# Graph-layer stack, one core: scores for four heads in one phase, a slope column in the weights, and sums of two key tiles for the products with ones

## The reference

```python
# layer 0: one GAT head, width 128, slope 0.2;  layer 3: four GAT heads of width 256 and an output GAT, slope 0.01
Wh = x @ W;  f, g = Wh @ a[0], Wh @ a[1]          # one number for each node
e = leaky_relu(f[:, None] + g[None, :]);  e = where(adj > 0, e, -1e9)
out = softmax(e) @ Wh
# layer 1: ordinary attention, 8 heads of width 32
scores = (q @ k.T) / sqrt(32);  scores = where(adj == 0, -inf, scores)
out = softmax(scores) @ v;  out = out @ Wo.T + bo
# layer 2: degree * (x @ Wi.T + b) + adj @ (x @ Wj.T)
# layer 3 goes on with elu, a two-layer FFN, a residual sum and a layernorm with gamma and beta
x = layernorm(x + layer(x))                        # four times
```

## Time and profile before

| what | before |
|---|---|
| median of 3 runs | 3322.02 us (3321.67 to 3324.13) |
| profiled execution, its own time | 3321.83 us |
| its span, first to last instruction | 3320.0 us |
| mean granted TensorE clock | 0.947 |
| PE busy | 2850.9 us, 86% |
| DVE busy | 2056.8 us, 62% |
| ACT busy | 1230.9 us, 37% |
| POOL busy | 811.2 us, 24% |

### The profile page before, as it was taken

The page is one execution under the profiler, slowest core; times in us unless marked ns, Lnnn a source line. Parts: engine busy times, 40 slices in busy tenths (PEclk is TensorE's granted clock), DMA queues, the critical chain, the costliest instruction groups (busy, mean ns, idle before and its releaser), DMA issues. The chain is left out here.

```text
span 3320.0 us, 47744 instructions
## 1 busy us (share of the span) xinstructions
PE 2850.9 (86%) x17559; PEld 2092.7 (63%) x17668; DVE 2056.8 (62%) x5644; ACT 1230.9 (37%) x2273; POOL 811.2 (24%) x640
## 2 busy tenths in 40 slices
PE   0779989898898989899898998989898898989876
PEld 0456666667666676676657666665766666676664
DVE  3447574766747576574857658485665848567453
ACT  0224334352433434343343434334243433424332
POOL 0112131412213132221313222131322213131221
PEclk9689999999999989989999999999999999989987
DMA  3000000000000000000000000000000000000000
GB/s 115 7 14 1 14 7 1 20 1 13 7 12 9 1 20 1 13 7 7 14 1 20 1 14 7 7 14 1 18 3 14 7 7 13 1 7 8 1 7 7
DMA packets 29764, 36.75 MB, mean 11 GB/s; under 512 B 2272, under 2 KB 23648, under 8 KB 29536
## 3 DMA queue, kind: packets, MB, share of 16 engines
q1 hardware_dynamic: 29536, 33.69, 3.2%
HBM read 25.30 MB, written 8.39 MB: 10 GB/s over the span
## 5 line engine op out<-in xcount | busy, mean ns | idle before, releaser
L465 POOL TENSOR_TENSOR exp_b<-exp_b,edge_t 128x512 int32<-128x512 int32 x320 | 433.8, 1363 | 1394.0 <-DVE exp_b L1057 1394.0
L580 PE MATMUL bank<-vals_b,exp_b 128*128 128x257 f32 x2560 | 632.9, 393 | 31.6 <-POOL exp_b L465 27.7
L580 PEld LDWEIGHTS bank<-vals_b,exp_b 128*128 128x128 f32 x2560 | 474.7, 193 | 158.9 <-POOL exp_b L465 51.5
L916 ACT ACTIVATE h_sb<-bank,rden_g_b 128x256 f32<-128x256 f32 x320 | 151.5, 474 | 719.1 <-DVE rden_g_b L1214 719.1
L1057 DVE TENSOR_TENSOR exp_b<-exp_b,low_b 128x512 f32<-128x512 f32 x320 | 294.0, 931 | 150.7 <-ACT low_b L832 150.3
L1070 DVE CUSTOM_DVE_ANT_0 picked<-bank,edge_bias 128x512 bf16<-128x512 f32 x512 | 327.2, 684 | 39.5 <-PE bank L598 39.1
L864 ACT ACTIVATE exp_a<-bank 128x512 f32<-128x512 f32 x512 | 277.0, 605 | 200.2 <-remote 122.6
L811 ACT ACTIVATE vals_b<-bank 128x512 f32<-128x512 f32 (+1 forms) x192 | 101.8, 545 | 536.2 <-PE bank L777 309.2
L1036 DVE CUSTOM_DVE_ANT_0 picked_b<-bank,edge_bias 128x512 bf16<-128x512 f32 x320 | 201.8, 686 | 102.4 <-PE bank L554 102.4
L649 PE MATMUL bank<-qk 32*128 32x512 f32 x1536 | 249.2, 428 | 16.9 <-ACT max_rows L811 12.2
L1114 DVE RECIPROCAL o_t<-bank 128x512 f32<-128x512 f32 x32 | 107.4, 3358 | 208.0 <-PE bank L672 208.0
(11 more groups left out here) (185 smaller groups left out, 5619.8 us busy)
## 6 DMA issues: line engine op xcount, KB each, us to landing
x_t<-in_x_t SPq DMA_DIRECT2D x16, 512.0 KB, 3.6
xa<-in_x SPq DMA_DIRECT2D x16, 512.0 KB, 3.8
out<-h_sb SPq DMA_DIRECT2D x16, 512.0 KB, 2.8
exp_b<-in_adj SPq DMA_DIRECT2D x1, 1024.0 KB, 7.0
edge_t<-in_adj_t SPq DMA_DIRECT2D x1, 1024.0 KB, 9.2
wo_sb<-in_L_gnn_W_out SPq DMA_DIRECT2D x1, 1024.0 KB, 11.7
ht_all<-in_L_gnn_a_heads SPq DMA_DIRECT2D x4, 256.0 KB, 8.7
exp_a<-in_L_gnn_W_heads SPq DMA_DIRECT2D x2, 512.0 KB, 4.2
```

Of the source, the lines that this page charges most:

```text
L465: pool.tensor_tensor(high_exp(idx, j).bitcast(I32), high_exp(idx, j).bitcast(I32), edge_t[:, j, :], ALU.mult)\
L580: last = pe.matmul(bank(key)[:, i * width:(i + 1) * width], high_exp(idx, c)[:, t * P:(t + 1) * P], vals[:, c, 0:width], start=c == 0, sto ...
```

## The change

- `st` holds all four heads of a group: four banks, twelve products L649, four rows, four masks. `mx` stays at two heads.
- In the odd key tiles POOL adds the exponentials of tiles t-1 and t of each head into `pair_sum`, and PE multiplies ones by `pair_sum`, in the odd `pv` phases only. ACT waits for these additions before it writes over the exponentials of two tiles ago. The additions of tile 3 wait until PE has read those of tile 1 (`summed`).
- The weights get one more column, slope times the column for g (set up once), so the product gives slope times g too. `shrunk_g` becomes `rounded_g`, one copy for all heads.
- `row_maxima` writes the masked row back to its own PSUM bank; one `picked` remains for the GAT rows.
- Some setup tensors share memory with others, and `TURNS` is another string.

Core of the diff:

```diff
+AT_ONCE = {"mx": 2, "st": 4}
-        V0, V3 = H0 + 3, F + 3
-        w0_sb = sb("w0_sb", [P, KF, H0 + 2])
-        wo3_sb = sb("wo3_sb", [P, H3 * KF, F + 2])
+        V0, V3 = H0 + 4, F + 4
+        w0_sb = sb("w0_sb", [P, KF, H0 + 3])
+        wo3_sb = sb("wo3_sb", [P, H3 * KF, F + 3])
+        pair_sum = sb("pair_sum", [P, HG, N])
-        picked = {s: sb("picked_" + s, [P, 2, N], BF16) for s in ("0", "10", "11", "b")}
+        picked = sb("picked", [P, 2, N], BF16)
...
@@ pool, mid_stream
+                for g in range(G1):
+                    for t in range(1, T, 2):
+                        for p in parts["st"]:
+                            yield "st", g, t, p
+                            for hh in heads_of("st", p):
+                                pool.wait_ge(*after(b, moved(("st", g, t, hh))))
+                                if t == T - 1:
+                                    pool.wait_ge(*after(b, sig.value("summed", g)))
+                                else:
+                                    for count in earlier(b, product_of(("sum", (g - 1) % G1), 0 if g else -1)):
+                                        pool.wait_ge(*count)
+                                pool.tensor_tensor(pair_sum[:, hh, :], exp1(g, t - 1, hh), exp1(g, t, hh), ALU.add)\
+                                    .then_inc(sig.raised("pair_added", (g, t // 2, hh)), 1)
@@ pe, scores
-                    heads = (2 * p, 2 * p + 1)
+                    heads = heads_of("st", p)
@@ pe, weigh
-                    for hh in range(HG):
-                        at = slice(hh * D1, (hh + 1) * D1)
-                        last = pe.matmul(bank(("sum", g))[at, :], ones[:], exp1(g, t, hh), start=t == 0, stop=t == T - 1)
+                    last.then_inc(filled(("o", g)) if t == T - 1 else sig.raised("weighed", (g, t)), 1)
+                    if t % 2:
+                        for hh in range(HG):
+                            at = slice(hh * D1, (hh + 1) * D1)
+                            pe.wait_ge(*after(b, sig.value("pair_added", (g, t // 2, hh))))
+                            last = pe.matmul(bank(("sum", g))[at, :], ones[:], pair_sum[:, hh, :], start=t == 1, stop=t == T - 1)
+                        last.then_inc(filled(("sum", g)) if t == T - 1 else sig.raised("summed", g), 1)
@@ act, exps and exps1
-                act.activation(low_exp(idx, j), bank(("low", idx))[:], ACT.Exp, bias=scaled_g[:, idx, j:j + 1])\
+                act.activation(low_exp(idx, j), bank(("low", idx))[:], ACT.Exp, bias=f_and_g(idx)[2][:, j:j + 1])\
+                        if old >= 0:
+                            if hh == 0:
+                                act.wait_ge(*after(b, product_of(("o", old // T)) if old % T == T - 1 else sig.value("weighed", (old // T, old % T))))
+                            act.wait_ge(*after(b, sig.value("pair_added", (old // T, old % T // 2, hh))))
@@ dve
-            def shrunk_g(b, first, last):
-                s, slope = stream_and_slope(first)
-                for i in range(first, last):
-                    dve.tensor_scalar(scaled_g[:, i, :], f_and_g(i)[1], slope, None, ALU.mult)\
-                       .then_inc(sig.raised("scaled_g_" + s, i), 1)
-                    dve.tensor_copy(g_r[:, i, :], f_and_g(i)[1]).then_inc(sig.raised("g_r_" + s, first) if i == last - 1 else
-                                                                          sig.raised("g_part_" + s, i), 1)
+            def rounded_g(first, last, g):
+                s = stream_and_slope(first)[0]
+                dve.tensor_copy(g_r[:, first:last, :], g).then_inc(sig.raised("g_r_" + s, first), 1)
-                    dve.tensor_tensor_reduce(picked[f"1{g}"][:, hh % 2, :], bank(key)[:], edge_bias[:, t, :], 1.0, START_MAX,
+                    dve.tensor_tensor_reduce(bank(key)[:], bank(key)[:], edge_bias[:, t, :], 1.0, START_MAX,
                                              ALU.add, ALU.max, max_c[:, g, t, hh:hh + 1]).then_inc(emptied(key), 1)
```

More of the change, by code:

```diff
@@ L175, in gat_mix_program, with heads_of @@
         ah_bc = ht_all[:].rearrange("p a n -> p (a n)")[:, 0:H3 * 2 * F].rearrange("p (h j f) -> p h j f", j=2, f=F)
+        A_END = 2 * H0 + 2 * F
+        first_row = a_bc[:, A_END:A_END + P]
+        wa = a_bc[:, A_END + P:A_END + P + KF * 3 * H3].rearrange("p (k c) -> p k c", k=KF)
         adj_i = exp_b[:, SLOTS - T:SLOTS, :].bitcast(I32)
         banks = [ctx.enter_context(nc.psum_tensor(f"bank{i}", [P, 512], F32)) for i in range(8)]
-        PAIRS = range(HG // 2)
+        def heads_of(kind, p):
+            w = AT_ONCE[kind]
+            return range(w * p, w * p + w)
+        parts = {kind: range(HG // w) for kind, w in AT_ONCE.items()}
         phases = {
@@ L189, in gat_mix_program @@
         }
-        phases["mid"] += [("mx", 0, t, p) for t in range(T) for p in PAIRS] + [("mr", 0)]
-        phases["second"] = [("q", 1)] + [("mx", 1, t, p) for t in range(T) for p in PAIRS] + [("mr", 1)]
+        phases["mid"] += [("mx", 0, t, p) for t in range(T) for p in parts["mx"]] + [("mr", 0)]
+        phases["second"] = [("q", 1)] + [("mx", 1, t, p) for t in range(T) for p in parts["mx"]] + [("mr", 1)]
         for g in range(G1):
             for t in range(T):
-                phases["mid"] += [("st", g, t, p) for p in PAIRS] + ([("pv", g, t - 1)] if t else [])
+                phases["mid"] += [("st", g, t, p) for p in parts["st"]] + ([("pv", g, t - 1)] if t else [])
             phases["mid"] += [("pv", g, T - 1), ("on", g)]
@@ L360, in gat_mix_program @@
         N_DOTS = 2 * KF + 2 * H3 * KF + 2 * H3 * KF
-        N_CONST = 9
+        N_CONST = 12
         small_loads = []
@@ L644, in scores @@
                             pe.wait_ge(*count)
-                    parts = [("k_hi", "q_hi"), ("k_hi", "q_lo"), ("k_lo", "q_hi")]
-                    for i, (k_part, q_part) in enumerate(parts):
+                    products = [("k_hi", "q_hi"), ("k_hi", "q_lo"), ("k_lo", "q_hi")]
+                    for i, (k_part, q_part) in enumerate(products):
                         for hh in heads:
@@ L683, in mid_stream @@
                 for t in range(T):
-                    for p in PAIRS:
+                    for p in parts["mx"]:
                         yield "mx", 0, t, p
@@ L858, in exps1 @@
                 def exps1(g, t, p):
[L859 to L863, removed]
+                    for hh in heads_of("st", p):
+                        key, old = ("st", g, t, hh), g * T + t - 2
+                        act.wait_ge(*after(b, product_of(key)))
+                        if old >= 0:
+                            if hh == 0:
+                                act.wait_ge(*after(b, product_of(("o", old // T)) if old % T == T - 1 else sig.value("weighed", (old // T, old % T))))
+                            act.wait_ge(*after(b, sig.value("pair_added", (old // T, old % T // 2, hh))))
+                        elif hh == 0:
+                            act.wait_ge(*after(b, product_of("a01")))
                         act.activation(exp1(g, t, hh), bank(key)[:], ACT.Exp, scale=SCALE1).then_inc(emptied(key), 1)
```

68 lines of the change are left out of this document (31 added, 37 removed).

## The result

| what | before | after |
|---|---|---|
| median | 3322.21 us (3321.67 to 3324.13, 4 runs) | 3200.73 us (3199.04 to 3204.11, 4 runs) |
| profiled execution; its span | 3321.83; 3320.0 us | 3200.4; 3198.6 us |
| PE busy; idle in the span | 2850.9; 469.1 us | 2670.4; 528.2 us |
| POOL busy | 811.2 us | 1136.5 us |
| mean granted TensorE clock | 0.947 | 0.950 |

The account below looks back on a forecast made before the run. PE was taken as the bound, busy 86% of the span. From 3321.8 us the terms -155 - 55 - 18 + 1 + 48 - 40 gave 3103 us, 6.6% faster; own range 3060 to 3160, stated range 3020 to 3240.

Parts of the forecast that it names:

- -155 for four heads: st phases: four row groups run together, saving 1.21 us in each of 128 phases, 155 us; ends -155 and -12.
- Work taken from PE counts in full, as long as no wait takes its place: Premise for the whole kernel: PE is the bound, busy 86% of the span, its many small waits none dominant.
- -55 for the ones: Ones products over pair sums: 64 of 128 blocks of 0.86 us go, saving 55 us.
- +48 for new waits: POOL's additions at pv0.3, pv1.3 and a3.3.0: some 3 us of PE waits a step, 48 us; ends 0 and +128.
- -40 for the order: Turn and end of the step: waits for xu_lo and low_b shrink, 2.5 us a step, 40 us; ends 0 and -80.
- -18 for the slope column: After fg: seven small DVE operations fewer shorten PE's wait for g_r, saving 18 us; ends -8 and -22.
- 0 for the masked row: row_maxima writing to PSUM: no cost seen by PE; DVE's price put between 0 and 126 us.
- The waits grow: Rival: less cover for the ACT, DVE, POOL, PE chains, 6 us more a step, 3199 us (3160 to 3290); chance 0.24.
- three signs of being wrong: Sixteen st products over 1.6 us, PE's idle share over 14%, or mean of L1057 (DVE) over 1.2 us.
- Slower by collisions: Rival: POOL's additions and DVE hold each other up, 1.1 us for each addition, 3385 us; chance 0.08.
- Only pairs: Rival: the array runs only pairs of row groups in st, 143 us of gain missing, 3246 us; chance 0.03.

Follow-up runs that it names:

- e13: The changed kernel without POOL's additions (e1), with two heads in an st phase again, the two phases one behind the other: 3253.84 us.
- e3: The changed kernel with two heads in an st phase again, the two phases one behind the other: 3261.09 us.
- e4: The kernel before with four heads in an st phase and nothing else, first of each two st turns taken out: 3262.36 us.
- e2: The changed kernel without POOL's additions, ones multiplied with the odd tiles alone, so sums leave out the even tiles: 3143.39 us.
- e1: The changed kernel without POOL's additions, ones multiplied with the exponentials of each key tile again: 3162.77 us.
- e15: The changed kernel, additions kept, with ab3.2 ab3.3 ahead of st1.1, ab0.2 ab0.3 ahead of e.0, norm3 behind norm0: 3125.12 us.
- e9: The changed kernel with phases ab3.2 and ab3.3 moved ahead of st1.1, so their cuts precede the additions on POOL: 3134.31 us.
- e14: The changed kernel without additions (e1), with ab0.2 ab0.3 ahead of e.0 and norm3 behind norm0: 3133.08 us.
- e16: The kernel with the moves of both e9 and e14 (e15), without POOL's additions: 3144.93 us.
- e8: The changed kernel with the order of phases of the kernel before, each pair of st phases made one: 3366.65 us.
- e5: The changed kernel without additions (e1), with the masked row of each maximum written to SBUF as bf16 again: 3149.13 us.
- e17: The changed kernel with additions and the moves of e15, the masked row written to SBUF as bf16 again: 3115.45 us.

## Why the prediction came out as it did

- **Direction, range and most of PE's work: right.** Four heads run together (2.00 us for a phase), the ones line fell from 135.1 to 74.3 us, POOL rose to 1136.5. In PE's busy time the whole brought 180.5 us, not 209. Most of the 28.5 us is a term that the sum did not have: the products of `mx`, which the change leaves as they are, went from 122.6 to 145.6 us (+23). `attend` is busy longer as well, from 632.9 to 659.6 us on exp_b and from 68.1 to 90.9 on exp_a, with the granted clock during these products down from 0.978 to 0.949 and from 0.892 to 0.775. Other products got that back: over all of PE's busy time the granted clock is 0.951 before and 0.949 after.
- **"-155 for four heads": the right price for the phases, too much for the kernel.** The phases gave the 155 (419.0 to 264.0), `mx` took 23 of it back, PE's work fell by about 125, and the time by 60 in the kernel after. "Work taken from PE counts in full, as long as no wait takes its place" was the sentence that carried this term; e13, e3 and e4 show that waits took a part in every order.
- **"-55 for the ones": worth about 19 alone (e2 against e1); with its additions it costs 38** in the order of the change. That was not priced as a pair. In the order of e15 the pair brings 20, or 8 against the best order without it.
- **"+48 for new waits": the place was right, the size not, and the cause was halved.** st1.2 waits 0.93 us (1.2 said), the ones 0.04 a step (0.2 said for each group). But a3.3.0 waits 3.60 where 1.5 was said, and the additions were charged with 0.6 of it: DVE's input for the first cut is ready 2.8 us before POOL starts it. The additions came 0.66 us late in themselves, and the clock fell behind the gap. e9, 66 us, is the price of that one queue order; as the same move costs 12 us without additions (e14 to e16), it is theirs in full.
- **"-40 for the order": the step that failed most plainly.** The waits that go did go (xu_lo 35.8, low_b 14.2 us). What stands behind them was not costed: four cuts of ab0 now come last ahead of a0 (2.46 us a step) and norm3 stands ahead of norm0, so x1 waits 4.82 us and not 3.00. Yet e8 shows that with the old order the change would lose 46 us, so as a whole the order was worth 166 us to this change (3366.65 - 3200.73), far beyond the 80 that bounded the term.
- **"-18 for the slope column": nothing.** g_r's wait went from 22.5 to 21.2 us. The prediction read it at the wrong place: it stands at the g of the output head, where the copy to g_r (from `vals_b`) comes behind a copy of ACT, and not behind the four pairs after fg. Those were also replaced by one copy of 1.22 us.
- **"0 for the masked row": 10 to 14 us** (e5, e17), within its bounds.
- **The rivals.** "The waits grow" is what came, by the mechanism it named, less cover for the chains. That its 3199 meets the measured 3200.73 is luck: it set 6 us a step for waits alone, and what came was 4.3 a step of waits (69.1/16) and 28.5 us of work. None of the prediction's three signs of being wrong showed (16 products in 1.12 us, PE idle for 12.8% of the middle, 850 ns), while it was 98 us off: they were set too wide to catch this. "Slower by collisions" did not decide: L1084's mean is 850 ns, below the 931 of before, and the additions' 1338. But its idea, an addition exposed in a row, is what e8 shows in the old order. "Only pairs" is refuted.

## What to carry to other kernels

Where one merged order binds in-order queues, price a new operation by what is queued behind it, and price a saving by the wait that stands next: here 100 to 125 us of TensorE's work were worth 56 to 91, and two phases moved were worth 66. Judge a part only in an order made for it, and so the kernel without it too: the additions cost 38 us in one order and brought 20 in another, and 8 when each side had its best measured order. Before an order is called a gain for the waits that it removes, list for each moved phase what comes later now.

## What was not expected of the hardware

- A small copy can take as long as a whole POOL operation. The 128x16 copy to g_r has a shortest of 176 ns and a median of 1220, when POOL's add runs beside it:

```profile
L1050 DVE CAST g_r<-fg_b x16: 176/1220/1240, 244.0 to 3052.0; 128x16 fp32r<-128x16 f32 x16
```
```profile
1557.98 2.48 POOL L469 TENSOR_TENSOR xbb<-xb,beta_bc 128x512 f32<-128x512 f32 x2 [1.98 <-DVE h_sb L1273]
```

  The copy starts 0.08 us after the first of two adds of 1.24 us and ends with it. The Trainium skill, "SBUF — State Buffer", section "Who interferes with whom", says that a copy in SBUF can enter a mode in which DVE and GpSimd lock each other out for a whole instruction; the trace agrees. Before, eight small operations there took 0.7 us together (1613.07 to 1613.74), so one copy of 1.22 us replaced them.
- DVE's write of its result to PSUM makes the read of the accumulator behind it slower too, 143 ns and not 83.
- The clock falls behind the same 3.1 us gap in each of fifteen steps, but by different amounts, 0.50 in three windows and 0.72 to 0.81 in twelve, with the same order of work. In e9, where the gap is gone, it is 1.00 there in all fifteen.
